# A decoder layer on one core: keys projected already turned, halves exchanged by DMA, and scores clipped by VectorE ahead of the exponential

## The chip, the core and the metric

The kernel runs on one core of one Trainium2 chip. TensorE (PE) multiplies matrices and writes to PSUM, eight banks of 512 fp32 numbers for each of 128 partitions. VectorE (DVE) and ScalarE (ACT) read and write PSUM and SBUF, GpSimd (POOL) only SBUF, and SyncE (SP) issues most of the transfers between memories. Each engine works through its own list of instructions in order and waits at semaphores for the others. The metric is the device time of one execution in microseconds; less is better.

## The reference

One decoder layer on x of 4 batches x 256 tokens x 128 features: local attention with relative positions, cross attention to a context of 512 tokens per batch, and a mixture of 12 experts, each added to x. The change touches the cross attention alone, which is, with 16 heads of 64:

```
lat = layer_norm(x);  ctx = layer_norm(context)          # with learned gain and bias
q = lat @ Wq;  k, v = split(ctx @ Wkv)                   # 16 heads of 64
k = concat([k1 * cos - k2 * sin, k2 * cos + k1 * sin])   # k1, k2: the halves of a head's 64
attn = clip(q @ k.T * 64 ** -0.5, -11, 11)
out = softmax(attn) @ v
x = x + out @ Wo + bo
```

## The kernel before

The program is written by hand, engine by engine, and the order of each engine's list is the order of the code. After the local attention comes a loop of 32 **rounds**, one for each pair of heads of a batch (8 pairs in each of 4 batches). In all engines' code the round is `r`, and a pair `p` has two halves of the context, `i = 2p` and `2p + 1`.

In round r, TensorE computes the scores of the *next* pair (`scores(2r+2)`, `scores(2r+3)`, two PSUM banks each, 128 x 1024 numbers), projects one **value unit** (128 context tokens x 8 heads, three matmuls of 512 columns, bank 5), in even rounds projects queries for the next two pairs (`queries`), weights the values by this pair's exponentials (`weigh_values(2r)`, `weigh_values(2r+1)`), sums the exponentials with a matrix of ones (`sum_weights(r)`), and projects one **key unit** (128 context tokens x 8 heads). Some rounds have an extra: the turn of a new batch's context or latents (the normed x), or an output projection (`project`). The value units run four ahead of the round in which they are first needed.

Keys arrive with tokens on the partitions. VectorE multiplies them from PSUM by cos and, halves swapped, by sin (`key_unit`, three instructions), GpSimd adds the two (`key_sum`), TensorE turns four 128 x 128 blocks for each pair (`turn_keys`) and ScalarE copies the result out of PSUM as `kT` (`keys_turned`). Queries, contexts, latents, projections and turned keys all share bank 6 (`MISC_BANK`), one after the other, with the semaphores `misc_ps` (written) and `misc_read` (read).

The scores go from PSUM through ScalarE, which writes their exponential to SBUF (`exponent`), and VectorE limits that in place (`clip`). GpSimd adds the halves of the exponentials (`weights_summed`, `halves_summed`). VectorE's `divide(r-1)` takes the reciprocal of the sums of the pair before and multiplies the weighted values by it. In VectorE's list, each round begins with it:

```
for r in range(NPAIR):
    if r:
        divide(r - 1)
    ...
    if r + 1 < NPAIR:
        clip(2 * r + 2)
        clip(2 * r + 3)
```

Between the division and the clips stand, in a few rounds, the statistics and normalizing of the next batch's latents (`latents`) and of the last norm (`final_norm`). After the loop come the experts, which the change leaves as they are.

Of the kernel before, what the change touches and what calls it, by code (L numbers as in the profile page):

```python
# [23 lines left out]
def decoder_layer(nc, x, ctx_in, pos, a_wq, a_wk, a_wv, a_wpost, a_wrel, a_pds,  # L24
# [52 lines left out]
    E_LO, E_HI = float(np.exp(-11.0)), float(np.exp(11.0))  # L77
    K_LEAD, V_LEAD = 2 * KC - 1, KC
# [21 lines left out]
    with ExitStack() as ctx:  # L100
# [17 lines left out]
        WARM_BANK, WARM_FIRST, WARM_NEXT = 6, 10, 4  # L118
# [21 lines left out]
        def bank(i, parts=P):  # L140
# [24 lines left out]
        ctx_sb = sb("ctx_sb", [P, NCT, D], F32, cross)  # L165
        ctx_f = sb("ctx_f", [P, SC], F32, cross)
# [3 lines left out]
        rope_a = sb("rope_a", [P, 2, GC], F32, cross)  # L170
        rope_b = sb("rope_b", [P, 2, GC], F32, cross)
        wkv_hi = sb("wkv_hi", [P, 2 * HX * DX], F32R, cross)
        wkv_lo = sb("wkv_lo", [P, 2 * HX * DX], F32R, cross)
        cos_sb = sb("cos_sb", [P, KC, DX // 2], F32, cross)
        sin_sb = sb("sin_sb", [P, KC, 2, DX // 2], F32, cross)
        k_rot = [sb(f"k_rot{i}", [P, KC, GC], F32, cross) for i in range(2)]
        raws = [raw[:, 0, :], raw[:, 1, :]] + [k_rot[1][:, t, :] for t in range(KC)]
# [29 lines left out]
        oT = sb("oT", [P, WALL * CH], F32, first)  # L207
        first.close()
# [9 lines left out]
        kT = sb("kT", [P, 3, SC], F32, second)  # L218
# [50 lines left out]
            rstd_done xn_done absneg_done softplus_done qscale_done awT_ps awT_done xT_ps xT_done v_tok_ps v_tok_done pad_set v_zeroed v_padded v_stored v_spread0 v_spread1 v_spread2  # L269
            rel_ps relM_done q_ps k_ps qM_done kM_done bd_ps bd_raw_done added_done pT_ps pT_done logit_ps  # L270
            capped_done prob_done oa_ps rq_done oq_done oT_ps oT_done ya_ps x1_done w_hi_done w_lo_done ctxn_done sin_done
            ct_ps ctx_f_done ctx_hi_done ctx_lo_done unit_ps rope_done v_done
            xn1_done lat_in_done lat_ps lat_f_done lat_hi_done lat_lo_done             k_rot_done misc_ps misc_read score_ps exp_done
            clip_done part_done es_done pv_ps den_ps rden_done ox_done tail_ps x2_done ld_w0 ld_w1 ld_w2 ld_w3
            ld_pw ld_u ld_b2 wt_done wt_hi_done wt_lo_done rt_ps rt_done fn_done fT_ps fT_done addr_ps addr_done z_ps
# [11 lines left out]
        UNIT = [("k", n) for n in range(KC)] + [("v", 0), ("v", 1), ("k", KC), ("k", KC + 1), ("v", 2), ("v", 3), ("k", KC + 2)]  # L287
        UNIT_BANK = [7, 6, 7, 6, 7, 6, 7, 6, 7, 7, 5]
        ROUND_VALUES, ROUND_KEYS = {}, {}
        for r in range(NPAIR):  # L290
            if r + V_LEAD < NG * KC:
                ROUND_VALUES[r] = len(UNIT)
                UNIT.append(("v", r + V_LEAD))
            if r + K_LEAD < NG * KC:
                ROUND_KEYS[r] = len(UNIT)
                UNIT.append(("k", r + K_LEAD))
        UNIT_BANK += [5] * (len(UNIT) - len(UNIT_BANK))

        def bank_before(m):

            n = m - 1
            while n >= 0 and UNIT_BANK[n] != UNIT_BANK[m]:
                n -= 1
            return n

        LATENT_ROUNDS = {1: (0, 1, 2), 2: (9, 10, 11), 3: (14, 15, 16)}
        CONTEXT_ROUND = {0: 1, PPB - 2: 2, 2 * PPB - 2: 3}
# [7 lines left out]
        MISC_BANK = 6  # L315
        MISC = [("keys", 0), ("queries", 0), ("keys", 1), ("keys", 2)]
        for r in range(NPAIR):
            if r in CONTEXT_ROUND:
                MISC.append(("context", CONTEXT_ROUND[r]))
            if r % 2 == 0 and r // 2 + 1 < NQ:  # L320
                MISC.append(("queries", r // 2 + 1))
            if r in extras:
                MISC.append(extras[r])
            if r + 3 < NPAIR:
                MISC.append(("keys", r + 3))
        MISC_NO = {what: n for n, what in enumerate(MISC)}

# [4 lines left out]
        def pv_bank(p):  # L332
# [4 lines left out]
        LAST_KEYS, LAST_VALUES = NG * KC - 1 - K_LEAD, NG * KC - 1 - V_LEAD  # L337
        NORM_ROUND = (B - 1) * PPB - 2
        ROUTE = {"weights": 2 * NORM_ROUND, "tokens": 2 * NORM_ROUND + 2, "address": 2 * NORM_ROUND + 4, "scores": 2 * NORM_ROUND + 6,
                 "chosen": 2 * NORM_ROUND + 8, "softmax": 2 * NORM_ROUND + 10, "turn": 2 * NORM_ROUND + 12}  # L340
        ROUTE_READ = {"weights": ("rt_done", 2), "tokens": ("fT_done", 1), "address": ("addr_done", 1), "scores": ("z_done", 1)}
# [33 lines left out]
        def _(sp):  # L375
# [24 lines left out]
            sp.dma_start(cos_sb[:, :, :], rope_cos.rearrange("(t p) d -> p t d", p=P)).then_inc(s["ld_rope"], 16)  # L400
            sp.dma_start(sin_sb[:, :, 1, :], rope_sin.rearrange("(t p) d -> p t d", p=P)).then_inc(s["ld_rope"], 16)
# [32 lines left out]
            sp.dma_start(pw_sb[:, :], f_pw).then_inc(s["ld_pw"], 16)  # L434
            for i, u in enumerate((f_u1, f_u2, f_u3)):
                sp.dma_start(u_sb[i * NE:(i + 1) * NE, :], u).then_inc(s["ld_u"], 16)
# [19 lines left out]
            for n in range(2 * NE):  # L456
                for g in GATE_AT.get(n, ()):
                    if GLOADS[g][1] == 1:
                        store_gates(GLOADS[g][0])
                    load_gates(g)  # L460
                if n >= RING:
                    sp.wait_ge(s["wt_done"], n - RING + 1)
                for j in range(P // SQ):
# [7 lines left out]
                    sp.dma_start(dst, src).then_inc(s[f"ld_w{n % RING}"], 16)  # L471
            for t in range(NT):
# [6 lines left out]
        def _(pool):  # L479
# [23 lines left out]
            link(pool.tensor_tensor(mask4[:, :], mask8[:, 0:G], mask8[:, G:HA], ALU.add))  # L503
            pool.memset(v_pad[:, :, 0:DA], 0.0).then_inc(s["pad_set"], 1)
# [8 lines left out]
            rstd_of(LN_C, KC)  # L513
            pool.memset(bd[:, :, :], 0.0).then_inc(s["consts"], 1)
# [13 lines left out]
            def key_sum(k):  # L528

                g, t = divmod(k, KC)  # L530
                pool.wait_ge(s["rope_done"], k + 1)
                if g >= 2:
                    pool.wait_ge(s["misc_ps"], MISC_NO["keys", GP * (g - 1) - 1] + 1)
                pool.tensor_tensor(k_rot[g % 2][:, t, :], rope_a[:, k % 2, :], rope_b[:, k % 2, :], ALU.add).then_inc(s["k_rot_done"], 1)  # L534

            def weights_summed(i):

                p, half = divmod(i, 2)
                pool.wait_ge(s["clip_done"], i + 1)
# [12 lines left out]
            weight_rest(1)  # L552
            key_sum(0)
            key_sum(1)
            weight_rest(2)
            key_sum(2)
            weight_rest(3)
            key_sum(3)
# [10 lines left out]
            for k in range(KC, KC + 2):  # L569
                key_sum(k)  # L570
# [18 lines left out]
            key_sum(K_LEAD - 1)  # L589
            for r in range(NPAIR):  # L590
# [10 lines left out]
                if r in ROUND_KEYS:  # L601
                    key_sum(r + K_LEAD)
# [27 lines left out]
        def _(act):  # L630
            act.dma_start(x_sb[:, NT // 2:NT, :], x[B // 2:B].rearrange("b (t p) d -> p (b t) d", p=P)).then_inc(s["ld_x1"], 16)
            act.dma_start(pds_b[:, 0, :], a_pds.partition_broadcast(P)).then_inc(s["ld_pds"], 16)
            act.dma_start(pos_sb[:, :], pos).then_inc(s["ld_pos"], 16)
            act.preload_act_table(ACT.Exp)
# [13 lines left out]
            act.wait_ge(s["absneg_done"], 1)  # L648
# [12 lines left out]
            act.wait_ge(s["qscale_done"], 1)  # L661
# [27 lines left out]
            def context_f(b):  # L689
                if b >= 1:  # L690
                    act.wait_ge(s["ctx_lo_done"], b)
                act.activation(ctx_f[:, :], bank(7 if b == 0 else MISC_BANK), ACT.Identity, scale=affine[:, 2:3], bias=affine[:, 3:4])\
# [49 lines left out]
            for i in range(2):  # L742
                shift_positions(act, 1, i)
            value_unit(4)
# [133 lines left out]
            for r in range(NPAIR):  # L878
# [18 lines left out]
                if r + 3 < NPAIR:  # L897
                    keys_turned(r + 3)
# [943 lines left out]
```

## Time and profile before

| | us |
|---|---|
| median of three runs | 442.74 (442.21 to 443.37) |
| the profiled execution | 443.53 |
| its span, first to last instruction | 441.6 |

| engine | busy us | share of the span | instructions |
|---|---|---|---|
| TensorE | 423.2 | 96% | 3210 |
| VectorE | 325.0 | 74% | 686 |
| ScalarE | 195.5 | 44% | 312 |
| GpSimd | 257.4 | 58% | 225 |

The durations further down come from the profiled execution. Its time is that of the whole execution, and the span is what the profiler saw of it. Matmuls overlap in TensorE's pipeline, so the time that a group of them takes is read from the starts of neighbouring groups. An engine's idle time counts only where something that ends later waits for it.

### The profile page before, as it was taken

The numbers are of one execution on the slowest core, as the hardware profiler recorded it, in microseconds if no ns is written. First come the engines' busy times: TensorE is split into PE (matmuls) and PEld (weight loads), VectorE is DVE, ScalarE is ACT, GpSimd is POOL, SyncE is SP. The second block draws the span as 40 slices with busy tenths as digits, with TensorE's granted clock in tenths as the row PEclk, the third lists the DMA queues.
The fourth block names the chain that finished last, engine by engine and source line by source line (L and its number), as shares of the span: only waits on it lengthen the run. The fifth ranks groups of instructions, "written<-read, shape, count | busy, mean of one in ns | idle before, by whom it ended". The sixth has DMA issues, their size and how long they took to land.

```text
span 441.6 us, 8547 instructions
## 1 busy us (share of the span) xinstructions
PE 423.2 (96%) x3210; PEld 313.1 (71%) x3210; DVE 325.0 (74%) x686; ACT 195.5 (44%) x312; POOL 257.4 (58%) x225
## 2 busy tenths in 40 slices
PE   8988799999999999999999999999999999999996
PEld 8666666676667766767776666768767788888885
DVE  8998658978869767985777698797687861755554
ACT  6848364646455346362535554534437634000000
POOL 5858238998778867878769665677524850000000
PEclk9999999999999999999999999999999999999999
DMA  7766405000000000000000000435518660000000
GB/s 178 202 150 90 85 18 87 1 0 1 1 1 1 1 1 1 1 0 1 2 1 1 1 1 1 154 63 94 122 29 212 143 98 0 6 7 12 6 7 13
DMA packets 75434, 19.85 MB, mean 45 GB/s; under 512 B 66741, under 2 KB 73834, under 8 KB 75394
## 3 DMA queue, kind: packets, MB, share of 16 engines
q1 hardware_dynamic: 72628, 18.27, 19.6%
q10 hardware_dynamic: 2766, 1.04, 1.1%
q8 instruction: 26, 0.43, 0.4%
q14 instruction: 14, 0.11, 0.1%
HBM read 17.27 MB, written 2.02 MB: 44 GB/s over the span
## 4 chain that ended last, share of the span: by engine, by line
PE 76%; DVE 11%; ACT 5%; issue 4%; DMA 1%; ACTq 1%; POOL 1%; DVEq 0%; POOLq 0%
PE psum L1199 11%; PE psum L1182 11%; PE psum L992 9%; PE psum L1382 5%; PE psum L1383 5%; PE psum L1381 5%; PE psum L1341 4%; PE psum L1342 4%; PE psum L1343 4%; PE psum L1218 3%; PE psum L1209 3%; PE psum L1101 3%; PE psum L941 1%; ACT e_sb L806 1%; DVE rden L1607 1%
## 5 line engine op out<-in xcount | busy, mean ns | idle before, releaser
L542 POOL TENSOR_TENSOR e_part<-e_sb 128x512 f32<-128x512 f32 x64 | 89.1, 1410 | 42.1 <-DVE e_sb L1600 30.4
L806 ACT ACTIVATE e_sb<-psum 128x1024 f32<-128x1024 f32 x64 | 62.2, 1022 | 16.7 <-PE psum L1182 16.7
L1182 PE MATMUL psum<-q_t,kT 64*128 64x256 f32 x512 | 64.2, 389 | 0.0
L1199 PE MATMUL psum<-e_sb,v_sb 128*64 128x256 f32 x512 | 63.8, 386 | 0.0
L1806 DVE SCALAR_TENSOR_TENSOR x_sb<-psum,dw,x_sb 128x128 f32<-128x128 f32 x96 | 33.7, 351 | 37.4 <-PE psum L1383 34.8
L1607 DVE RECIPROCAL rden<-psum 128x256 f32<-128x256 f32 x32 | 55.8, 1745 | 0.2 <-PE psum L1209 0.2
L1600 DVE TENSOR_SCALAR e_sb<-e_sb 128x1024 f32<-128x1024 f32 x64 | 51.4, 839 | 3.8 <-ACT e_sb L806 3.8
L1182 PEld LDWEIGHTS psum<-q_t,kT 64*128 64x128 f32 x512 | 46.7, 186 | 9.6 <-issue 5.0
L785 ACT ACTIVATE kT<-psum 128x512 f32<-128x512 f32 x32 | 19.1, 598 | 77.7 <-PE psum L1101 77.3
L1199 PEld LDWEIGHTS psum<-e_sb,v_sb 128*64 128x64 f32 x512 | 33.7, 136 | 22.3 <-issue 6.6
L534 POOL TENSOR_TENSOR k_rot<-rope_a,rope_b 128x512 f32<-128x512 f32 x32 | 41.7, 1307 | 12.8 <-DVE rope_b L1487 12.8
L582 POOL TENSOR_TENSOR xeT_lo<-xeT,xeT_hi 128x512 fp32r<-128x512 f32 x24 | 31.6, 1318 | 28.0 <-ACT xeT_hi L820 27.9
L1482 DVE TENSOR_TENSOR rope_a<-psum,cos_sb 128x512 f32<-128x512 f32 x32 | 22.1, 690 | 28.8 <-PE psum L992 26.6
L548 POOL TENSOR_TENSOR e_part<-e_part 128x512 f32<-128x512 f32 x32 | 41.4, 1293 | 2.5
L1341 PE MATMUL psum<-xeT_hi,w1T_hi 128*128 128x512 f32 x96 | 38.9, 405 | 0.8 <-ACT h_f L926 0.5
L1382 PE MATMUL psum<-w2T_lo,h_hi 128*128 128x512 f32 x96 | 38.0, 396 | 0.0
L1383 PE MATMUL psum<-w2T_hi,h_lo 128*128 128x512 f32 x96 | 37.8, 394 | 0.0
L1343 PE MATMUL psum<-xeT_hi,w1T_lo 128*128 128x512 f32 x96 | 37.5, 390 | 0.0
L1342 PE MATMUL psum<-xeT_lo,w1T_hi 128*128 128x512 f32 x96 | 37.5, 390 | 0.0
L1381 PE MATMUL psum<-w2T_hi,h_hi 128*128 128x512 f32 x96 | 37.3, 389 | 0.0
L992 PE MATMUL psum<-wkv_hi,ctx_hi 128*128 128x512 f32 x64 | 31.5, 493 | 2.8 <-DVE rope_b L1487 2.7
L820 ACT ACTIVATE xeT_hi<-xeT 128x512 fp32r<-128x512 f32 x24 | 15.2, 631 | 28.7 <-DVE xeT L1647 21.3
(195 smaller groups left out, 780.8 us busy)
## 6 DMA issues: line engine op xcount, KB each, us to landing
w_raw<-in_L_ffn_W_dram SPq DMA_DIRECT2D x96, 64.0 KB, 2.4
gates<-gate_dram SPq DMA_DIRECT2D x6, 768.0 KB, 4.9
ctx_sb<-in_ctx_dram SPq DMA_DIRECT2D x4, 256.0 KB, 6.2
vbd<-v_dram SPq DMA_DIRECT2D x16, 52.6 KB
v_dram<-v_tok SPq DMA_DIRECT2D x4, 136.0 KB, 3.3
raw<-in_L_xattn_Wkv_dram SPq DMA_DIRECT2D x2, 256.0 KB, 4.5
k_rot<-in_L_xattn_Wkv_dram SPq DMA_DIRECT2D x2, 256.0 KB, 5.3
k_rot<-in_L_xattn_Wq_dram SPq DMA_DIRECT2D x2, 256.0 KB, 5.7
```

The source lines that it names most:

```text
L542: pool.tensor_tensor(e_part[:, p % 2, half, :, :], e_sb[:, i % ERING, :, 0, :], e_sb[:, i % ERING, :, 1, :], ALU.add)\
L806: act.activation(e_sb[:, i % ERING, :, :, :].rearrange("p a k t -> p (a k t)"), psum[:, a:a + 2, :].rearrange("p a b -> p (a b)"), ACT.Exp ...
L992: mm = pe.matmul(o, c, w_[:, wc:wc + GC], start=(part == 0), stop=(part == 2))
L1182: mm = pe.matmul(psum[:, 2 * (i % 2) + a, t * S:(t + 1) * S], kT[rows, p % 3, kt * P:(kt + 1) * P], q_t[rows, j % 2, p % 2, :], start=True ...
L1199: mm = pe.matmul(psum[DX * a:DX * a + DX, pv_bank(p), 0:S], v_sb[g % 2][:, kt, 2 * pp + a, :], e_sb[:, i % ERING, a, t, :], start=(kt == 0 ...
L1341: pe.matmul(bank(c), w1T_hi[:, e, c, :], hi, start=(e == 0), stop=False)
L1342: pe.matmul(bank(c), w1T_hi[:, e, c, :], lo, start=False, stop=False)
L1343: mm = pe.matmul(bank(c), w1T_lo[:, e, c, :], hi, start=False, stop=(e == NE - 1))
L1381: pe.matmul(o, hi, w_hi, start=(c == 0), stop=False)
L1382: pe.matmul(o, hi, w_lo, start=False, stop=False)
L1383: mm = pe.matmul(o, lo, w_hi, start=False, stop=(c == HC - 1))
L1607: dve.reciprocal(rden[:, p % 2, :], psum[:, pv_bank(p), S:2 * S]).then_inc(s["rden_done"], 1)
```

## The change

Keys. A key unit is now one pair of heads x 512 context tokens, with the weights as the stationary operand, so that PSUM receives the keys already turned. The tables of cos and sin are turned once at the start (`rope_t`, 32 small transposes). VectorE makes both products in one instruction of 1024 numbers (`key_products`). The sin product has to move to the other half of each head, which is now another partition: for the first four pairs TensorE does that with a permutation matrix and VectorE adds (`first_key_sum`), and for the other 28 four DMAs on SP's queue do it, and GpSimd adds into `kT`, a ring of four (`key_sum`). The turns of keys and ScalarE's copies of them are gone.

Scores. VectorE clips the scores from PSUM into SBUF, and ScalarE takes the exponential there in place.

Banks. Key units of the loop use bank 6. Queries, contexts, latents and projections use bank 5, where the value units are (`aside`, two of them excepted).

```diff
-    K_LEAD, V_LEAD = 2 * KC - 1, KC
+    S_CLIP = 11.0 / X_SCALE
+    K_LEAD, V_LEAD = 4, KC
+    KRING = 4
...
+                VALUES_BEFORE[what] = min(r + 1 + V_LEAD, NG * KC)
...
+            def swap_keys(p):
+
+                sp.wait_ge(s["rope_done"], 2 + p + 1)
+                sp.wait_ge(s["k_done"], p - 1)
+                for q in range(2 * DX // QD):
+                    to = q ^ 1
+                    sp.dma_start(raw[QD * to:QD * (to + 1), p % 2, :], rope[QD * q:QD * (q + 1), p % 2, 1, :]).then_inc(s[f"ld_raw{p % 2}"], 16)
...
             def exponent(i):
-                act.wait_ge(s["score_ps"], i + 1)
...
+                act.wait_ge(s["clip_done"], i + 1)
+                e = e_sb[:, i % ERING, :, :, :].rearrange("p a k t -> p (a k t)")
+                act.activation(e, e, ACT.Exp, scale=X_SCALE).then_inc(s["exp_done"], 1)
...
             for r in range(NPAIR):
                 if r + 1 < NPAIR:
                     exponent(2 * r + 2)
+                if ASIDE[r] and r in ROUND_VALUES:
+                    value_unit(ROUND_VALUES[r])
+                if r + 1 < NPAIR:
                     exponent(2 * r + 3)
+                if not ASIDE[r] and r in ROUND_VALUES:
+                    value_unit(ROUND_VALUES[r])
+                for what in ASIDE[r]:
+                    aside(what)
...
                 if MISC_NO[what]:
                     pe.wait_ge(s["misc_read"], MISC_NO[what])
+                if what in VALUES_BEFORE:
+                    pe.wait_ge(s["v_done"], VALUES_BEFORE[what])
...
+                    unit_values(ROUND_VALUES[r])
+                if r in ROUND_KEYS:
+                    unit_keys(ROUND_KEYS[r])
+                for what in ASIDE[r]:
+                    aside(what)
+                route_1(2 * r)
                 weigh_values(2 * r)
...
             def clip(i):
 
-                dve.wait_ge(s["exp_done"], i + 1)
-                e = e_sb[:, i % ERING, :, :, :].rearrange("p a k t -> p (a k t)")
-                dve.tensor_scalar(e, e, E_LO, E_HI, ALU.max, ALU.min).then_inc(s["clip_done"], 1)
+                dve.wait_ge(s["score_ps"], i + 1)
...
+                a = 2 * (i % 2)
+                dve.tensor_scalar(e_sb[:, i % ERING, :, :, :].rearrange("p a k t -> p (a k t)"), psum[:, a:a + 2, :].rearrange("p a b -> p (a b)"),
+                                  -S_CLIP, S_CLIP, ALU.max, ALU.min).then_inc(s["clip_done"], 1)
```

How this moves instructions is shown at three places. `v_done` counts the value units that ScalarE has copied out. First TensorE's list from the end of one round into one with a query projection (`q_t` of L1115 before, L1157 after), before the change:

```order
L992 MATMUL psum<-wkv_hi,ctx_lo 128x512
L1101 MATMUL psum<-ident,k_rot 128x128 [waits misc_read,k_rot_done]
L1101 MATMUL psum<-ident,k_rot 128x128 x3
L1182 MATMUL psum<-q_t,kT 128x256 [waits exp_done,misc_read]
L1182 MATMUL psum<-q_t,kT 128x256 x3
L1182 MATMUL psum<-q_t,kT 128x256 [waits exp_done]
L1182 MATMUL psum<-q_t,kT 128x256 x3
L992 MATMUL psum<-wkv_hi,ctx_hi 128x512 [waits ctx_lo_done,rope_done]
L992 MATMUL psum<-wkv_lo,ctx_hi 128x512
L992 MATMUL psum<-wkv_hi,ctx_lo 128x512
L1115 MATMUL psum<-lat_hi,wq_hi 128x256 [waits misc_read,lat_lo_done]
```

and the same place after it (L1010 to L1012 is the value unit, L1031 to L1033 the key unit):

```order
L1226 MATMUL psum<-q_t,kT 128x256 [waits clip_done,k_done,misc_read]
L1226 MATMUL psum<-q_t,kT 128x256 x3
L1226 MATMUL psum<-q_t,kT 128x256 [waits clip_done]
L1226 MATMUL psum<-q_t,kT 128x256 x3
L1010 MATMUL psum<-wkv_hi,ctx_hi 128x512 [waits ctx_lo_done,misc_read,v_done]
L1011 MATMUL psum<-wkv_lo,ctx_hi 128x512
L1012 MATMUL psum<-wkv_hi,ctx_lo 128x512
L1031 MATMUL psum<-ctx_hi,wkv_hi 128x512 [waits ctx_lo_done,rope_done]
L1032 MATMUL psum<-ctx_hi,wkv_lo 128x512
L1033 MATMUL psum<-ctx_lo,wkv_hi 128x512
L1157 MATMUL psum<-lat_hi,wq_hi 128x256 [waits v_done,misc_read,lat_lo_done]
```

The four turns of keys are gone, the key unit stands behind the value unit, and the query projection has a new wait, for `v_done`. Second, ScalarE's list in two rounds, the second with a query projection, before:

```order
L806 ACTIVATE e_sb<-psum 128x1024 [waits part_done,pv_ps,score_ps] x2
L713 ACTIVATE v_sb<-psum 128x512 [waits pv_ps,unit_ps]
L785 ACTIVATE kT<-psum 128x512 [waits score_ps,misc_ps]
L806 ACTIVATE e_sb<-psum 128x1024 [waits part_done,pv_ps,score_ps] x2
L713 ACTIVATE v_sb<-psum 128x512 [waits pv_ps,unit_ps]
L798 ACTIVATE q_t<-psum 128x512 [waits score_ps,misc_ps]
L785 ACTIVATE kT<-psum 128x512 [waits score_ps,misc_ps]
```

and after (each `e_sb` is an exponential, `v_sb` the copy of a value unit):

```order
L811 ACTIVATE e_sb<-e_sb 128x1024 [waits clip_done]
L730 ACTIVATE v_sb<-psum 128x512 [waits pv_ps,unit_ps]
L811 ACTIVATE e_sb<-e_sb 128x1024 [waits clip_done]
L806 ACTIVATE q_t<-psum 128x512 [waits score_ps,misc_ps]
L811 ACTIVATE e_sb<-e_sb 128x1024 [waits clip_done]
```

The copy of the value unit now stands between the two exponentials of the round, and these wait for clips, where they waited for scores. Third, VectorE's list of one round, before:

```order
L1607 RECIPROCAL rden<-psum 128x256 [waits ox_done,den_ps]
L1611 TENSOR_TENSOR o_t<-psum,rden 128x256 [waits rden_done]
L1600 TENSOR_SCALAR e_sb<-e_sb 128x1024 [waits exp_done] x2
L1482 TENSOR_TENSOR rope_a<-psum,cos_sb 128x512 [waits k_rot_done,unit_ps]
L1487 TENSOR_TENSOR rope_b<-psum,sin_sb 128x8x32 x2
```

and after (`den_ps` counts TensorE's `sum_weights`):

```order
L1662 RECIPROCAL rden<-psum 128x256 [waits ox_done,den_ps]
L1666 TENSOR_TENSOR o_t<-psum,rden 128x256 [waits rden_done]
L1654 TENSOR_SCALAR e_sb<-psum 128x1024 [waits part_done,pv_ps,score_ps] x2
L1531 TENSOR_TENSOR rope<-psum,rope_t 128x1024 [waits k_done,unit_ps]
L1662 RECIPROCAL rden<-psum 128x256 [waits ox_done,den_ps]
```

The places are the same, but the clips now come between the scores and the exponentials, and one instruction stands where the three products of keys stood.

## Rows read from the trace of the kernel before

**Rows 1.** The page, busy time, share of the span and instructions of TensorE.

```profile
PE 423.2 (96%) x3210; PEld 313.1 (71%) x3210; DVE 325.0 (74%) x686; ACT 195.5 (44%) x312; POOL 257.4 (58%) x225
```

**Rows 2.** Windows, rounds 0 to 27: length, engines' busy time in their order, granted clock, DMA.

```profile
60.72:270.75 210.03, 205.00 (x1482) 142.41 (x1482) 166.82 (x295) 105.71 (x154) 166.74 (x132) 1.00 0.04 6
```

**Rows 3.** The chain that ended last: start, us, what.

```profile
60.72 1.06 PE psum L1182 x8
...
145.35 1.98 PE psum L1218 x16
...
270.75 1.93 PE psum L1182 x16
```

**Rows 4.** Timeline of a round without extras, all engines.

```profile
97.65 0.69 DVE L1482 TENSOR_TENSOR rope_a<-psum,cos_sb 128x512 f32<-128x512 f32 x1 [1.69 <-PE psum L992]
...
97.98 2.00 PE L1182 MATMUL psum<-q_t,kT 64*128 64x256 f32 x16
...
98.92 1.75 DVE L1607 RECIPROCAL rden<-psum 128x256 f32<-128x256 f32 x1
99.17 1.94 ACT L806 ACTIVATE e_sb<-psum 128x1024 f32<-128x1024 f32 x2 [0.48 <-PE psum L1182]
...
99.91 0.50 PE L992 MATMUL psum<-wkv_hi,ctx_hi 128*128 128x512 f32 x1
...
100.71 0.42 DVE L1611 TENSOR_TENSOR o_t<-psum,rden 128x256 f32<-128x256 f32 x1
...
100.79 1.95 PE L1199 MATMUL psum<-e_sb,v_sb 128*64 128x256 f32 x16
...
100.99 0.60 ACT L713 ACTIVATE v_sb<-psum 128x512 f32<-128x512 f32 x1
101.05 1.28 DVE L1600 TENSOR_SCALAR e_sb<-e_sb 128x1024 f32<-128x1024 f32 x2
...
102.57 0.60 PE L1209 MATMUL psum<-e_part,ones 128*64 128x256 f32 x4
...
103.10 0.50 PE L992 MATMUL psum<-wkv_hi,ctx_hi 128*128 128x512 f32 x1
...
104.43 2.00 PE L1182 MATMUL psum<-q_t,kT 64*128 64x256 f32 x16
```

**Rows 5.** Timeline of a round with a query projection, TensorE: its start and what follows.

```profile
122.08 0.28 PE L1115 MATMUL psum<-lat_hi,wq_hi 128*128 128x256 f32 x1
...
122.88 1.95 PE L1199 MATMUL psum<-e_sb,v_sb 128*64 128x256 f32 x16
```

**Rows 6.** Line L1600: count, duration min/median/max in ns, first and last start.

```profile
L1600 DVE TENSOR_SCALAR e_sb<-e_sb x64: 660/685/2229, 57.4 to 287.7; 128x1024 f32<-128x1024 f32 x64
```

**Rows 7.** Groups by line: count, us in all, mean ns, idle before.

```profile
L1496 DVE TENSOR_SCALAR kM<-psum,mask 128x512 f32<-128x512 f32 x8 | 8.5, 1185 | 1.0 <-PE psum L963 1.0
```

**Rows 8.** Timeline of a round with a context turn.

```profile
107.44 0.78 ACT L692 ACTIVATE ctx_f<-psum,affine 128x512 f32<-128x512 f32 x1
...
108.36 0.36 PE L1115 MATMUL psum<-lat_hi,wq_hi 128*128 128x256 f32 x1 [0.64 <-ACT ctx_f L692]
...
108.92 1.56 DVE L1472 TENSOR_TENSOR ctx_lo<-ctx_f,ctx_hi 128x512 fp32r<-128x512 f32 x1
```

**Rows 9.** The chain at the last sums of the loop.

```profile
294.00 0.58 PE psum L1209 x4
```

**Rows 10.** Timeline of VectorE behind these sums.

```profile
294.63 1.76 DVE L1607 RECIPROCAL rden<-psum 128x256 f32<-128x256 f32 x1
```

**Rows 11.** Timeline of VectorE's work for the latents in one round.

```profile
176.25 0.59 DVE L1425 TENSOR_SCALAR xn<-x_sb,mv,rstd 128x128 f32<-128x128 f32 x2
...
177.56 1.26 DVE L1600 TENSOR_SCALAR e_sb<-e_sb 128x1024 f32<-128x1024 f32 x2
```

**Rows 12.** DMA issues: count, KB each, median us from issue to landing.

```profile
w_raw<-in_L_ffn_W_dram SPq DMA_DIRECT2D x96, 64.0 KB, 2.4
```

More of the change, by code:

```diff
@@ L551, in _ @@
             weight_rest(0)
[L552 to L558, printed above, removed]
+            for n in range(1, 4):
+                weight_rest(n)
             pool.wait_ge(s["added_done"], 1)
@@ L633, in _ @@
             act.dma_start(pos_sb[:, :], pos).then_inc(s["ld_pos"], 16)
+            for i, table in enumerate((rope_cos, rope_sin)):
+                act.dma_start(rope_in[:, i, :, :], table.rearrange("(t p) d -> p t d", p=P)).then_inc(s["ld_rope"], 16)
             act.preload_act_table(ACT.Exp)
@@ L875, in route_1, with aside @@
                     if ROUTE[stage] == i:
-                        route(0, stage, 5)
+                        route(0, stage, ROUTE_BANK.get(stage, 5))
+            def aside(what):
+                if what[0] == "context":
+                    misc_wait(what)
+                    context_f(what[1])
+                elif what[0] == "queries":
+                    queries_out(what[1])
+                elif what[0] == "latents":
+                    misc_wait(what)
+                    latents_f(what[1])
             for r in range(NPAIR):
@@ L893, in _ @@
                     final_normalize(0)
-                if r in extras and extras[r][0] == "latents":
-                    misc_wait(extras[r])
-                    latents_f(extras[r][1])
-                if r + 3 < NPAIR:
-                    keys_turned(r + 3)
+                for what in LATE[r]:
+                    aside(what)
                 route_1(2 * r + 1)
@@ L951, in _ @@
             turned(psum[:, 1, P:P + NPOS], pos_sb[:, :], NPOS).then_inc(s["awT_ps"], 1)
+            pe.wait_ge(s["ld_rope"], 32)
+            for i in range(2):
+                for t in range(KC):
+                    for q in range(2 * DX // QD):
+                        mm = turned(psum[QD * q:QD * (q + 1), 5 - i, t * P:(t + 1) * P], rope_in[:, i, t, :])
+                mm.then_inc(s["rope_ps"], 1)
             keep_clock(WARM_NEXT)
@@ L996, in relative, with swap_keys @@
+            def swap_keys(p):
+                if p == 0:
+                    pe.wait_ge(s["turn_set"], 2 * DX // QD + 2)
+                pe.wait_ge(s["rope_done"], 2 + p + 1)
+                pe.matmul(bank(UNIT_BANK[p]), swap[:, :], rope[:, p % 2, 1, :], start=True, stop=True).then_inc(s["rope_ps"], 1)
             def relative(c):
@@ L1289, in route_1, with aside @@
                     pe.wait_ge(s["rt_done"], 2)
+                if i == ROUTE["turn"]:
+                    pe.wait_ge(s["rope_done"], 2 + NPAIR)
                 for stage in ROUTE:
                     if ROUTE[stage] == i:
-                        route(0, stage, 5)
+                        route(0, stage, ROUTE_BANK.get(stage, 5))
+            def aside(what):
+                if what[0] == "queries":
+                    queries(what[1])
+                    return
+                misc_free(what)
+                if what[0] == "context":
+                    turn_context(what[1], 5, "misc_ps")
+                elif what[0] == "latents":
+                    turn_latents(what[1], 5, "misc_ps")
+                else:
+                    project(what[1], what[2], psum[:, misc_bank(what), 0:D]).then_inc(s["misc_ps"], 1)
             for r in range(NPAIR):
```

372 lines of the change are left out of this document (181 added, 191 removed).

## The prediction

> **What bounds the kernel now.** I read the page first. TensorE (PE) is busy 96% of the span, 423.2 us [rows 1], so the question for any stretch is whether something makes TensorE wait there. Next I cut the span at the starts of two score groups on the chain of waits, scores 2 at 60.72 and scores 58 at 270.75 [rows 3]. Between them lie rounds 0 to 27 of the cross attention, the rounds that the change touches most. They take 210.03 us, TensorE is busy 205.0 of them, VectorE (DVE) 166.8, and the granted clock is 1.00, the upper level of 2.4 GHz [rows 2]. So TensorE sets the pace there, and VectorE has about a fifth to spare.
>
> Then I read one round in the timeline [rows 4]. A round without extras runs from 97.98 to 104.43, 6.45 us: scores 1.93, a value unit until 100.79 (0.88 with the switch of operands), weighting by the exponentials 1.78, the two sums 0.53, a key unit and its four turns 1.33. What matters most here is who waits for whom. ScalarE (ACT) starts its exponentials at 99.17, as soon as scores are in PSUM. VectorE divides (reciprocal from 98.92), multiplies (100.71) and only then clips (101.05), but nobody needs those clips before the next round. So VectorE's slow reciprocal is on nobody's way. A round with a query projection has 0.80 more (122.08 to 122.88, [rows 5]).
>
> **The change, part by part.**
>
> *Removed from TensorE.* The key unit moves beside the value unit, and the four turns of keys go. A round without extras becomes 1.93 + 0.88 + 0.8 + 1.78 + 0.53, about 5.9 us instead of 6.45 [rows 4]: 0.6 us in each of 28 rounds, some 17 us, if nothing waits. ScalarE's copy of keys leaves its queue, and nothing waits for that space.
>
> *Clips from PSUM.* A clip of 1024 numbers in SBUF takes 685 ns in the median [rows 6]. From PSUM I go by two rows: a product of 256 numbers takes 0.42 us (100.71) and one of 512 takes 0.69 (97.65, both [rows 4]), so 0.27 us for each 256 more, and 1.23 us for 1024. The bounds are 0.685 below, and above twice the 1185 ns that the tensor-scalar operation from PSUM takes for 512 with a scattered output [rows 7], about 2.3 us. I take 1.24, because the new output is contiguous like that of the product. The Trainium skill, "VectorE: DVE Perf Modes", section "Mode 2×_2P — use both read ports for one tensor", says that the two-port mode which doubles a single-source operation is open only to SBUF, since VectorE has one read port on PSUM. By its rate of one element per cycle at 0.96 GHz, 1024 numbers are an estimated 1.1 us before overhead; with that the forecast below would be about 3 us lower. No row shows this very operation.
>
> *Key products and sums.* One product of 1024 from PSUM (1.24) stands for three that took from 97.65 to 98.92, 1.27 [rows 4]: nothing to count. GpSimd (POOL) adds as before.
>
> *Halves exchanged by DMA.* Four transfers of 64 KB per pair go through SP's queue. A 64 KB transfer lands 2.4 us after its issue [rows 12]; even four in sequence, 9.6 us, end inside the more than ten that lie between a key product late in one round and its sum at the end of GpSimd's next round. I count 0. What covers it is the four-slot ring of keys; with that cover gone it would be some 2 us a round. Expert loads behind it on SP wait for the end of the loop anyway.
>
> *The wait that is added.* The query projection (also a context turn, a latent turn or an output projection) now writes bank 5, where this round's value unit has just been put. So it waits for ScalarE's copy of that unit. In ScalarE's queue the copy stands behind the first exponential; that waits for the clip; and the clip stands behind the division in VectorE's queue, which waits for the sums at the end of TensorE's last round. Counted from the start of a round's scores:
> the reciprocal starts at 0.05 (294.58 to 294.63, [rows 9, 10]); the multiply 1.79 later; the clip 0.34 after that [rows 4]; 1.24 for the clip; 0.05 to hand over; 0.96 until ScalarE takes up its next instruction (half of 1.94, less overlap, [rows 4], with 0.04 for the SBUF source, an estimate); 0.60 for the copy, like the value copy at 100.99 [rows 4]; 0.14 until TensorE starts (context copy 107.44 + 0.78, then 108.36, [rows 8]). Together 5.17 us. TensorE itself is there at 1.93 + 0.88 + 0.8 = 3.6. It waits 1.6 us, and behind it in its queue are the weighting and the sums of this round, for which the next division waits. So the chain closes on itself once a round, and a round costs 5.17 + the extra + 1.78 + 0.53 = 7.48 + the extra.
>
> The sum over rounds 0 to 27:
> - 23 rounds with such an extra: 23 x 7.48 = 172.0.
> - The extras: 13 query projections x 0.80 = 10.4; three contexts and three latents x 0.4 (an estimate) = 2.4; five output projections x 1.98 [rows 3] = 9.9.
> - Round 0, taken like the others: 7.5. Rounds 5 and 9, without an extra: 11.7.
> - Rounds 23 and 25: a routing step waits for the value copy, which there stands behind both exponentials: 7.48 + 0.96 + 0.9 each, 18.7.
> - Work on VectorE ahead of the clips, now on the chain: statistics or normalizing of latents in seven of these rounds and once for the last norm. One such piece takes 176.25 to 177.56, 1.31 [rows 11]; 8 x 1.3 = 10.4. Until now VectorE's spare fifth held it.
> - Work behind the clips that waits for ScalarE or TensorE and so delays the next division: three contexts (first copy to remainder 1.48, then 0.7 to 1.56, [rows 8], and the key product, ending near 9.5 where the round ends at 8), three latents, two routing rounds: 8 x 1.5 = 12.0, the softest term.
>
> That is 255.0 against 210.0, +45. The time ahead of the loop: 64 small transposes of tables and four fp32 swaps come, six filler matmuls, seven key units' sums and a negation go; I take +1, bounds -2 and +3, since much of that stretch waits on DMA round trips. The rounds after 270.75 and the experts (156 us) are the same. So +46 on the profiled execution's 443.53 us gives 489.5; that execution lies 0.8 above the median of the three runs (442.74), so I predict **489 us**.
>
> **The rivals.**
> *Faster.* The copies come early enough and TensorE never waits. Then only the removed work shows: 255 less 23 x 1.6, 2 x 2.5 and the 22.4 of late work is 191, 19 less than now, and the time about 425 us. For it: TensorE is 97.6% busy in the loop [rows 2], and its removed work is real. Against: the copy would have to end by 3.6 us, and the reciprocal and multiply alone, 2.2 us [rows 4], with the exponential and the copy, 1.56, pass that without any clip. It decides only if the division does not stand ahead of the clip, which the order shows it does.
> *About the same.* The waits are half as long as I count (a clip at the SBUF price, and the late work mostly in gaps): 45 less 14 less 22 still leaves +9, so this needs two errors of mine together. 442 us.
> *Slower still, the clock.* In the loop the granted clock is 1.00 [rows 2], and the longest TensorE wait that my rows show is 0.64 us [rows 8]. With the change TensorE would wait 1.6 us in most rounds and 3 us in the seven with latents work. If the clock fell to its lower level (1.2 GHz) in those seven, their TensorE work of at most 6.3 us would double, up to +44; for half of each, +22, so about 510 us. The Trainium skill, "TensorE: Matmul & The Clock Gate", the table in "Why this matters for your kernels", says that idle gaps between bursts of matmuls bring the half rate back; no row of this loop shows one, so I give it little.
>
> **How the numbers follow.** Forecast (chain through the value copy) 0.83; clock on top 0.06; faster 0.08; same 0.03. A measurement of this kernel can tell about 0.3% from no change. Faster 0.08, same 0.03, slower 0.89. The range: a clip at 0.685 takes 25 x 0.55 = 14 off, late work half hidden 11; a clip at 2.3 adds 26; the clock adds 22. I take 468 to 510, which leaves out the faster and same cases and the outer ends.
>
> **What would show it.** Right: in the profile after, TensorE idle before the query projection with ScalarE's value copy as the releaser, 1.5 us or more, some 20 times; query rounds of 8.2 to 8.5 us; the reciprocal starting within 0.2 us of the sums; clips of 1.2 us; VectorE idle at the end of rounds; the turns of keys gone. Wrong: TensorE still over 95% busy in the loop; clips waiting for scores instead of for the division; copies released early; or waits at the key sums, which would mean that the DMA is late.

## The result, and the profile after

The changed kernel takes **518.4 us** (516.3 to 520.9, four runs) where the kernel before takes 442.6: 1.172 times as long (95% interval 1.169 to 1.175). The forecast was 489, with a range to 510. The profiled execution took 517.46 us, its span 515.7, 74.1 more than before. The page of the changed kernel, engines' busy times (to be read beside [rows 1]) and TensorE's granted clock in 40 slices of the span:

```profile
PE 437.1 (85%) x3148; PEld 316.1 (61%) x3148; DVE 339.6 (66%) x627; ACT 179.2 (35%) x280; POOL 238.4 (46%) x227
...
PEclk9899989789987898989999798899999999999999
```

TensorE is busy 85% of the span instead of 96%, and it does fewer matmuls for 14 us more of busy time, since part of them run at less than full clock. Windows of the changed kernel (columns as in [rows 2]): rounds 0 to 27, round 28, and the rest; then single rounds, 4, 5, 6 and 10.

```profile
66.43:339.09 272.66, 215.57 (x1376) 144.97 (x1375) 177.28 (x244) 91.56 (x127) 154.15 (x133) 0.91 0.13 31
339.09:349.82 10.73, 7.37 (x49) 4.45 (x47) 5.12 (x5) 3.77 (x5) 5.00 (x5) 0.84 0.10 25
349.82:515.70 165.88, 159.46 (x766) 124.86 (x764) 105.97 (x245) 46.34 (x80) 52.09 (x40) 1.00 0.30 64
```

```profile
104.73:115.44 10.71, 8.35 (x50) 5.53 (x48) 6.45 (x6) 3.09 (x4) 7.25 (x6) 0.84 0.20 50
115.44:121.26 5.82, 5.82 (x44) 3.86 (x42) 5.58 (x5) 2.24 (x3) 1.18 (x1) 1.00 0.01 1
121.26:129.63 8.37, 6.77 (x50) 4.63 (x48) 6.17 (x6) 3.45 (x5) 7.51 (x7) 1.00 0.18 46
154.48:168.76 14.28, 9.60 (x50) 6.05 (x48) 8.70 (x12) 4.08 (x6) 10.44 (x10) 0.77 0.15 38
```

The 74.1 us lie in three places: 5.7 ahead of the loop (66.43 less 60.72), 62.6 in rounds 0 to 27 (272.66 less 210.03), and 5.8 behind them. In the loop the granted clock is 0.91 where it was 1.00. Rounds 5 and 6, at a clock of 1.00, take 5.82 and 8.37, as forecast (5.9, and 7.48 + 0.80). Rounds 4 and 10, like round 6 with a query projection, take 10.7 and 14.3 at 0.84 and 0.77.

Round 6 in the timeline, to be read beside [rows 4, 5]:

```profile
121.26 2.00 PE L1226 MATMUL psum<-q_t,kT 64*128 64x256 f32 x16
121.38 1.76 DVE L1662 RECIPROCAL rden<-psum 128x256 f32<-128x256 f32 x1 [0.20 <-PE psum L1253]
...
123.51 2.34 DVE L1654 TENSOR_SCALAR e_sb<-psum 128x1024 f32<-128x1024 f32 x2
...
124.76 1.06 ACT L811 ACTIVATE e_sb<-e_sb 128x1024 f32<-128x1024 f32 x1 [3.14 <-DVE e_sb L1654]
125.72 0.58 ACT L730 ACTIVATE v_sb<-psum 128x512 f32<-128x512 f32 x1
...
126.45 0.36 PE L1157 MATMUL psum<-lat_hi,wq_hi 128*128 128x256 f32 x1 [1.60 <-ACT v_sb L730]
...
127.32 1.95 PE L1243 MATMUL psum<-e_sb,v_sb 128*64 128x256 f32 x16
```

This is the chain of the forecast, link by link: sums, reciprocal, multiply, clip, exponential, value copy, query projection. It takes 126.45 - 121.26 = 5.19 us (forecast 5.17), and TensorE waits 1.60. Round 10 in the timeline, where the normalizing and statistics of latents stand ahead of the clips:

```profile
162.75 0.55 PE L1157 MATMUL psum<-lat_hi,wq_hi 128*128 128x256 f32 x1 [4.68 <-ACT v_sb L730]
...
164.30 3.68 PE L1243 MATMUL psum<-e_sb,v_sb 128*64 128x256 f32 x16
...
167.77 1.07 PE L1253 MATMUL psum<-e_part,ones 128*64 128x256 f32 x4
...
168.88 1.76 DVE L1662 RECIPROCAL rden<-psum 128x256 f32<-128x256 f32 x1 [5.60 <-PE psum L1253]
```

TensorE waits 4.68 us, and behind the wait the same weighting that took 1.95 us in round 6 takes 3.68, and the sums 1.07 instead of 0.60: TensorE runs at its lower level. VectorE waits 5.60 us for these sums, so the chain, which closes on itself, carries the delay into the next round.

Groups by line of the changed kernel (busy us, mean ns, idle before), and last the transfers of the exchange (count, KB each, median us from issue to landing):

```profile
L811 ACT ACTIVATE e_sb<-e_sb 128x1024 f32<-128x1024 f32 x64 | 67.4, 1054 | 184.5 <-DVE e_sb L1654 184.0
L1662 DVE RECIPROCAL rden<-psum 128x256 f32<-128x256 f32 x32 | 56.1, 1754 | 61.8 <-PE psum L1253 61.7
L1654 DVE TENSOR_SCALAR e_sb<-psum 128x1024 f32<-128x1024 f32 x64 | 75.1, 1212 | 1.0 <-PE psum L1226 0.9
L1531 DVE TENSOR_TENSOR rope<-psum,rope_t 128x1024 f32<-128x1024 f32 x32 | 38.7, 1213 | 1.1 <-PE psum L1033 1.1
L557 POOL TENSOR_TENSOR kT<-rope,raw 128x512 f32<-128x512 f32 x28 | 35.5, 1269 | 0.0
...
raw<-rope SPq DMA_DIRECT2D x112, 64.0 KB, 2.0
```

Clips (1.21 us) and key products (1.21) cost what was forecast, and GpSimd never waits for the exchange by DMA (idle 0.0 ahead of the key sums). ScalarE waits 184 us for clips.

What remains open is the 17.6 us of the loop beyond the forecast's 45, and the 11.5 outside it. **Theory:** the chain is as long as forecast, and the rest of the loop's loss is the clock that falls behind the waits. **Rivals:** the chain itself is longer than the sum of its rows (work on VectorE ahead of it), and the low clock costs nothing, as TensorE waits anyway; VectorE is simply too full; or the keys part has a wait of its own.

### The profile page after: what moved, and what is told of

The parts are those of the page before. It is cut to its first block, busy times and chain, and to the rows that moved or that the text cites. A ratio compares the mean times of both kernels' runs of the same rounds, so it can differ in the third digit from the quotient of the medians.

```text
span 515.7 us, 8442 instructions
## 1 busy us (share of the span) xinstructions
PE 437.1 (85%) x3148; PEld 316.1 (61%) x3148; DVE 339.6 (66%) x627; ACT 179.2 (35%) x280; POOL 238.4 (46%) x227
## 4 chain that ended last, share of the span: by engine, by line
PE 58%; DVE 23%; issue 10%; ACT 7%; DMA 1%; SPq 0%; DVEq 0%; POOL 0%
PE psum L1243 11%; DVE rden L1662 7%; DVE e_sb L1654 6%; PE psum L1428 4%; PE psum L1429 4%; PE psum L1427 4%; PE psum L1226 4%; PE psum L1387 4%; PE psum L1262 3%; PE psum L1389 3%; PE psum L1388 3%; PE psum L1253 3%; ACT v_sb L730 2%; ACT e_sb L811 2%; PE psum L1157 2%
## 5 line engine op out<-in xcount | busy, mean ns | idle before, releaser
L565 POOL TENSOR_TENSOR e_part<-e_sb 128x512 f32<-128x512 f32 x64 | 82.0, 1288 | 122.9 <-ACT e_sb L811 109.4
L811 ACT ACTIVATE e_sb<-e_sb 128x1024 f32<-128x1024 f32 x64 | 67.4, 1054 | 184.5 <-DVE e_sb L1654 184.0
L1243 PE MATMUL psum<-e_sb,v_sb 128*64 128x256 f32 x512 | 77.0, 452 | 1.3 <-issue 1.2
L1654 DVE TENSOR_SCALAR e_sb<-psum 128x1024 f32<-128x1024 f32 x64 | 75.1, 1212 | 1.0 <-PE psum L1226 0.9
L1243 PEld LDWEIGHTS psum<-e_sb,v_sb 128*64 128x64 f32 x512 | 40.0, 159 | 27.0 <-issue 14.0
L1531 DVE TENSOR_TENSOR rope<-psum,rope_t 128x1024 f32<-128x1024 f32 x32 | 38.7, 1213 | 1.1 <-PE psum L1033 1.1
L1157 PE MATMUL psum<-lat_hi,wq_hi 128*128 128x256 f32 x32 | 11.7, 366 | 31.6 <-ACT v_sb L730 31.5
L557 POOL TENSOR_TENSOR kT<-rope,raw 128x512 f32<-128x512 f32 x28 | 35.5, 1269 | 0.0
L1157 PEld LDWEIGHTS psum<-lat_hi,wq_hi 128*128 128x128 f32 x32 | 7.1, 222 | 38.0 <-issue 36.8
L1262 PE MATMUL psum<-wo_sb,o_t 128*128 128x128 f32 x128 | 17.8, 299 | 10.5 <-issue 10.5
```

The lines of the kernel that those rows point to most:

```text
L565: pool.tensor_tensor(e_part[:, p % 2, half, :, :], e_sb[:, i % ERING, :, 0, :], e_sb[:, i % ERING, :, 1, :], ALU.add)\
L811: act.activation(e, e, ACT.Exp, scale=X_SCALE).then_inc(s["exp_done"], 1)
L1243: mm = pe.matmul(psum[DX * a:DX * a + DX, pv_bank(p), 0:S], v_sb[g % 2][:, kt, 2 * pp + a, :], e_sb[:, i % ERING, a, t, :], start=(kt == 0 ...
L1654: dve.tensor_scalar(e_sb[:, i % ERING, :, :, :].rearrange("p a k t -> p (a k t)"), psum[:, a:a + 2, :].rearrange("p a b -> p (a b)"), -S_C ...
```

## The experiments

**The value copy first** (e1).

```diff
-                if r + 1 < NPAIR:
-                    exponent(2 * r + 2)
-                if ASIDE[r] and r in ROUND_VALUES:
+                if r in ROUND_VALUES:
                     value_unit(ROUND_VALUES[r])
                 if r + 1 < NPAIR:
+                    exponent(2 * r + 2)
                     exponent(2 * r + 3)
-                if not ASIDE[r] and r in ROUND_VALUES:
-                    value_unit(ROUND_VALUES[r])
```

> One edit: in every round ScalarE copies the value unit before its two exponentials. Theory A (the loss is the chain through the value copy, division - clip - exponential - copy): TensorE finds bank 5 free at 3.6 us of a round, the wait of 1.6 us at the asides goes, and with it the drops of the granted clock that follow it; rounds of 6 us and 6.8 with a query, bound by TensorE and VectorE together (2.1 + 2.4 + 1.2 = 5.8 us of VectorE), loop 205 to 215 instead of 272.7, time 450 to 460. Rival B (VectorE is simply too full: clips of 1.21 from PSUM on top of the division, whoever waits for the copy): no change, 510 to 520. Rival C (the clock falls for another reason than the wait): TensorE's wait goes, but rounds at a clock of 0.7 to 0.87 stay, time near 480.

464.0 us (1.047, 1.043 to 1.051); loop 217.05, clock 0.98. The wait at the asides is gone, and 55.6 us of the loop's 62.6 with it, though VectorE does the same work: VectorE's load is not the main cause. The time is 4 us over what was expected. About 2 us of that lie in the loop, where a smaller wait took the place of the first, and the loop also starts 1.8 us later than in the changed kernel (68.21, against 66.43). The scores of this kernel in its groups by line (busy us, mean ns, idle before, and what ended it):

```profile
L1223 PE MATMUL psum<-q_t,kT 64*128 64x256 f32 x512 | 67.4, 404 | 11.0 <-ACT q_t L806 11.0
```

They wait 11.0 us, in seven rounds, for ScalarE's copy of the queries. It stands behind the second exponential, and so behind the second clip and the division; the next scores need it.

**The clips first** (e2).

```diff
+                if r + 1 < NPAIR:
+                    clip(2 * r + 2)
+                    clip(2 * r + 3)
                 if r:
                     divide(r - 1)
...
-                if r + 1 < NPAIR:
-                    clip(2 * r + 2)
-                    clip(2 * r + 3)
```

> One edit: in every round VectorE does both clips before the division (and the latents' statistics behind the division), ScalarE's order as in the changed kernel. Theory A: the division leaves the chain; clip 1 ends at 2.3 us of a round, the exponential at 3.3, the copy at 3.9, TensorE starts the aside at 4.05 instead of 5.2, being there at 3.6; loop 215 to 225, time 450 to 465, some 5 us more than with the copy first if nothing else differs, less if the work that stands ahead of the clips matters more. Rival B (VectorE too full): no change, since the same work stays in its queue, 510 to 520.

460.4 us (1.040, 1.035 to 1.045); loop 219.45, clock 0.98. With the division off the chain, the query projection waits for the value copy only 9.9 us in 15 rounds, 0.5 to 0.6 in most, as worked out.

**The keys part alone** (e3), with exponential and clip as in the kernel before; scores and weighting wait accordingly.

```diff
             def exponent(i):
-                act.wait_ge(s["clip_done"], i + 1)
+                act.wait_ge(s["score_ps"], i + 1)
...
             def clip(i):
-                dve.wait_ge(s["score_ps"], i + 1)
+                dve.wait_ge(s["exp_done"], i + 1)
```

> The keys part alone: keys projected turned and rotated from PSUM, exchanged by DMA, as in the changed kernel, but scores as before (exponential by ScalarE from PSUM, clip by VectorE in SBUF behind it). Theory A: the exponential no longer waits for the division, the copy ends at 3.5 us of a round, no wait; TensorE saves the turns of keys, 0.6 us a round; loop about 195, and with the 5.7 us lost ahead of the loop the time is 430 to 437, faster than the kernel before. Rival D (the keys part brings its own wait, at the DMA exchange or at bank 5): 450 or more, with waits at the scores for the key sums or at the asides.

**437.7 us, 0.988 (0.986 to 0.991): 1.2% less than before.** Windows, rounds 0 to 27, and round 27 alone:

```profile
65.34:264.73 199.39, 194.09 (x1376) 133.26 (x1375) 172.89 (x244) 91.77 (x127) 167.44 (x133) 0.99 0.18 43
```

```profile
252.44:264.73 12.29, 9.60 (x61) 6.90 (x59) 9.15 (x13) 2.54 (x3) 7.52 (x6) 0.86 0.15 38
```

The loop is 10.6 us shorter than before; in rounds 0 to 26 no wait of TensorE is longer than 0.73 us, and none is for the key sums or the DMA. So the loss of the whole change is that of the scores part. The time is just above the 430 to 437 expected, because of round 27, taken up below.

**The scores part alone** (e4), the kernel before with the reverse of that edit.

> The scores part alone: the kernel before with VectorE's clip from PSUM ahead of ScalarE's exponential in SBUF, keys as before. Theory A: the value copy stands behind both exponentials there and the key unit waits for it in bank 5, while VectorE's key products stand ahead of the next division; round of 2.2 + 2.4 + 1.05 + 0.75 + 0.65 + 1.3 = 8.4 us, loop 240 to 260 instead of 210, time 475 to 495. Rival D (the loss comes from the keys part or from its order of asides): near 443 to 450.

520.2 us (1.175, 1.172 to 1.178), as much as the whole change. A round with neither extra nor latents work takes 8.38 us, against 8.4 worked out; in the timeline of one (136.80 to 145.18) the key unit waits:

```profile
143.20 0.58 ACT L713 ACTIVATE v_sb<-psum 128x512 f32<-128x512 f32 x1
143.84 0.50 PE L988 MATMUL psum<-wkv_hi,ctx_hi 128*128 128x512 f32 x1 [1.82 <-ACT v_sb L713]
```

But the loop takes 282.7 at a clock of 0.90, far over the 240 to 260 expected, and the time misses its 475 to 495: here too the plain rounds come out and the rounds with long waits do not. How much of that is the waits themselves and how much the clock was not measured in this kernel.

**Both orders** (e5), the edits of e1 and e2 together.

> Both orders at once: ScalarE copies the value unit before the exponentials, and VectorE clips before it divides; the clip stays from PSUM. Each order alone left a wait of its own: with the copy first the next scores waited 1.3 to 2.5 us for ScalarE's copy of the queries (which stands behind the second exponential, behind the second clip, behind the division); with the clips first the asides waited 0.5 us for the value copy. Theory A (the chain): with both neither is left, query rounds of 6.85 us, loop 200 to 208 against 217.1 and 219.5, time 446 to 452. Rival B (a clip from PSUM ahead of the exponential has a price of its own, in VectorE's time, whatever the order): rounds stay at 7 us or more, time 456 or more.

449.8 us (1.018, 1.014 to 1.021); loop 207.20. Query rounds take 6.86 us, the same as with the keys part alone, where the clip is in SBUF and late. A clip from PSUM ahead of the exponential therefore costs nothing in a plain round once the orders suit it.

**TensorE kept at work while it waits** (e6). Repeats of a key unit's first matmul, 4 to 19 in each of 25 rounds (`FILL`), stand ahead of it; the unit then overwrites the bank.

```diff
+                for _ in range(FILL.get(p - K_LEAD, 0)):
+                    pe.matmul(o, wkv_hi[:, cols], ctx_hi[:, b % 2, :], start=True, stop=True)
                 pe.matmul(o, wkv_hi[:, cols], ctx_hi[:, b % 2, :], start=True, stop=False)
```

> The changed kernel with TensorE kept at work while it waits: ahead of the key unit of each of 25 rounds stand 4 to 19 repeats of its first matmul (0.22 us each, results overwritten by the unit), chosen to fill the measured wait of that round but for some 0.4 us. The chain through the value copy is left as it is. Theory C (beyond the chain, the loop lost 18 us because TensorE's granted clock falls after the waits and the projections, weightings and sums behind them run at half rate): the rounds that showed a clock of 0.72 to 0.87 show 0.95 or more and lose 1 to 3 us each; loop 252 to 257 instead of 272.7, which is the 255 that the chain gives; time 497 to 503, although 200 matmuls more are done. Rival A' (the chain alone is longer than counted, and the low clock costs nothing, since TensorE waits anyway): 515 to 522, no change.

**500.3 us (1.132, 1.130 to 1.134), 18 less than the changed kernel, with 200 matmuls more.** Windows, rounds 0 to 27, and rounds 4, 5, 6 and 10:

```profile
66.52:319.81 253.29, 239.69 (x1575) 170.98 (x1574) 178.42 (x244) 91.63 (x127) 154.38 (x133) 0.99 0.14 33
```

```profile
101.97:111.10 9.13, 8.81 (x59) 6.33 (x58) 6.54 (x6) 3.10 (x4) 5.70 (x5) 1.00 0.18 44
111.10:116.93 5.83, 5.83 (x45) 3.86 (x43) 5.58 (x5) 2.26 (x3) 2.75 (x3) 1.00 0.10 24
116.93:125.31 8.38, 7.93 (x56) 5.57 (x54) 6.18 (x6) 3.44 (x5) 7.51 (x7) 1.00 0.19 47
148.47:159.97 11.50, 11.08 (x70) 8.20 (x68) 8.84 (x12) 4.10 (x6) 8.97 (x9) 1.00 0.14 34
```

Rounds 4 and 10 come back to a clock of 1.00 and get shorter by 1.6 and 2.8 us; rounds 5 and 6, at 1.00 already, don't change by more than 0.01. The eleven rounds that get shorter by over 0.2 us (2, 4, 8, 10, 11, 13, 16, 22, 23, 25, 26) give 19.3 of the 19.4 between the two loops, and they are the rounds from 1 on in which the clock had fallen. The other 17 change by at most 0.04, though 14 of them hold repeats too, so the repeats do nothing where the clock was up. The loop that is left, 253.3 us, is the chain at a clock of 0.99 (only round 0 is still at 0.80), where the forecast had 255.0. This settles the loop: the rival, that the low clock costs nothing, would have shown no change.

**Two orders mended on the keys part alone** (e7): ahead of the loop, VectorE's statistics ahead of its table copies and GpSimd's clearing ahead of the swap matrix; in the loop:

```diff
-                if i in ROUTE.values():
+                if i in (ROUTE[stage] for stage in ROUTE if stage not in ("chosen", "softmax")):
                     pe.wait_ge(s["v_done"], min(r + 1 + V_LEAD, NG * KC))
                     pe.wait_ge(s["misc_read"], MISC_BEFORE[r] + len(ASIDE[r]))
```

> The keys part alone, with two orders mended. Ahead of the loop VectorE takes the statistics of the first context before its copies of the turned tables, and GpSimd clears its buffers before it makes the swap matrix; in the loop TensorE no longer waits at the two routing steps in which it has no work. Theory (the 5.7 us ahead of the loop come from the context's statistics and GpSimd's clearing coming late, so that the normalizing of the context meets GpSimd's work; and the 2.65 us of wait in round 27, with a clock of 0.86 behind it, come from that routing wait): the loop starts 2 to 3 us earlier than with the keys part alone, at 62 to 63.5 instead of 65.34, round 27 takes 8.5 to 9.5 instead of 12.29, time 431 to 434. Rival (the start is bound by the 64 transposes of the tables on TensorE; round 27 is bound by VectorE's routing work): 436 to 438.

433.0 us (0.981, 0.978 to 0.984). The profiled execution is the shortest of its four (428.9), so the mends were also run apart.

**The start alone** (e9), **the routing wait alone** (e10), each on the keys part.

> The keys part alone with only the two orders ahead of the loop mended (statistics of the first context ahead of the table copies, buffers cleared ahead of the swap matrix); the routing wait stays. With both mends the profiled execution, the shortest of its kernel (428.9 against a median of 433.0), started its loop at 61.50 instead of 65.34. Theory (these orders cost 2.5 us at turn_context, from 20.0 to 22.5): the context is turned 1.5 to 2.5 us earlier, the loop starts at 62 to 64, time 434 to 436. Rival (what starts the loop later stands behind, at the wait for the value copy near 40 us): the context is turned earlier, the loop starts at 65 as before, time 437 to 438.

> The keys part alone without the wait of TensorE at the two routing steps in which it has no work; the orders ahead of the loop stay. Theory: round 27 takes 8 instead of 12.29, the rest is as with the keys part alone; time 433 to 434. Rival: the wait goes to the next user of that PSUM bank, the value unit of round 28, and 437 stays.

The start alone: 436.4 us (0.986, 0.982 to 0.990), an interval that overlaps that of the keys part alone, so no gain is shown. The context is turned at 20.53 instead of 22.51, but the loop starts at 65.72, no earlier (e3: 65.34): in between, VectorE waits 2.65 us for a DMA of shifted positions where it waited 0.91. The routing wait alone: **433.4 us, 0.979 (0.976 to 0.982), 2.1% under the kernel before**, which is all that both mends gave. Window of round 27:

```profile
250.81:258.75 7.94, 7.89 (x60) 5.69 (x59) 7.80 (x20) 2.54 (x3) 5.07 (x5) 1.00 0.13 34
```

It takes 7.94 us instead of 12.29. There TensorE had waited 2.65 us at a stage in which only VectorE works, for a read of bank 5 that stands behind that work, and in e3 the weighting behind it ran at half rate. It did not in e9, behind the same wait, and the round took 10.59. The weighting in e3 and in e9:

```profile
260.73 3.31 PE L1247 MATMUL psum<-e_sb,v_sb 128*64 128x256 f32 x16 [2.65 <-issue]
```

```profile
261.31 1.95 PE L1247 MATMUL psum<-e_sb,v_sb 128*64 128x256 f32 x16 [2.65 <-issue]
```

**The whole change with all orders mended** (e8), the edits of e5 and e7 together.

> The whole change, scores part included, with all the orders mended at once: value copy ahead of the exponentials, clips ahead of the division, the two orders ahead of the loop, and no wait at routing steps in which TensorE has no work. Theory (the change loses by four orders, not by what its instructions cost): the 449.8 us of both orders together less 3.8 ahead of the loop (65.34 to 61.50 with the keys part alone), less 5.5 in round 27 (14.00 to 8.5) and 2 in round 28; 437 to 441, faster than the kernel before by about 1%, but behind the keys part alone with its orders mended (433), since VectorE's clips stay ahead of TensorE in the rounds with latents and routing work. Rival (the waits of rounds 23, 26 and 27 are VectorE's load there, not the routing wait): 444 or more.

446.7 us (1.009, 1.006 to 1.011): the expectation of 437 to 441 fell. Its loop is 200.95, but round 23 waits 2.51 us for ScalarE's copy of the routing weights, and a routing turn in round 28 waits 3.65, with a clock of 0.72 for that round, 11.95 us long. So in rounds with routing work the scores part still brings waits of its own, and of that part nothing was found that pays for it: with it the time is 446.7, without it, with the same two mends, 433.0 (e7).

## Why the prediction was wrong, by its steps

*Removed from TensorE.* Right: 5.82 us for a plain round (5.9), and alone this part makes the kernel 1.2% faster (e3).

*Clips from PSUM; key products; DMA.* Right: 1.21 us each, as counted (1.24), and the exchange is hidden (64 KB in 2.0 us). The estimate from the Trainium skill, "VectorE: DVE Perf Modes", section "Mode 2×_2P — use both read ports for one tensor", left out overhead and was 0.1 short; its rule agrees with the trace, in which the clip from PSUM takes 1.21 us and the clip in SBUF 0.69 (the median of [rows 6]).

*The wait that is added.* Right, in mechanism and size, where VectorE has no other work: in round 6 5.19 us from the start of the round to the projection (5.17), 1.60 us of wait. e1 and e2 each take one link out, and the wait goes or shrinks to 0.5. The rival "faster" (a loop of 191 us) comes near the keys part alone (199.39); what it needed, a copy that doesn't wait for the division, is what the scores part takes away.

*The sum over rounds 0 to 27.* Right at full clock: 253.3 measured in e6, 255.0 forecast. That it came so close is luck in part. The terms for late work were not measured apart, and single rounds were off by over 2 us either way, which cancels: for round 13 7.48 + 1.98 gives 9.5, and 11.9 came; for round 25 7.48 + 0.96 + 0.9 + 1.5 gives 10.8, and 8.7 came.

*The rival "slower still, the clock".* **This is the step that failed.** It named the mechanism and worked out 22 us, and then gave it 0.06, because "no row of this loop shows one". But that loop had no long waits to show: the longest was 1.06 us (round 0; the 0.64 is only the longest among the rows), and the forecast itself put waits of 1.6 and 3 us into it. It happened, and cost 19.4 us (272.66 less 253.29), in rounds spread over the loop and not only in those with latents.

In the changed kernel the granted clock stays at 1.00 behind the waits of 1.6 us (rounds 6 and 12), falls behind those of 2.36, 2.56, 3.06 and 4.68 (rounds 4, 8, 2 and 10), and does not behind those of 2.24 and 2.35 (rounds 14 and 18). The length of the wait alone does not decide it here: the clock stays up behind 2.85 us (rounds 1 and 15) and falls in the rounds of 1.78 and 2.00 us (25 and 11). Even the same wait goes both ways, as in e3 and e9 above. Ahead of the loop the first local values wait 2.82 us in all ten profiles with the new keys; they then take 2.2 us in four of them and 2.6 to 3.9 in six. The changed kernel (granted clock 1.00 in these values) and e3 (0.54):

```profile
43.99 2.21 PE L1106 MATMUL psum<-vbd,prT 96*32 96x68 f32 x128 [2.82 <-ACT v_sb L730]
```

```profile
42.66 3.74 PE L1110 MATMUL psum<-vbd,prT 96*32 96x68 f32 x128 [2.82 <-ACT v_sb L730]
```

So 19.4 us is what the clock cost in the profiled execution of the changed kernel, and not a fixed price of its waits. The Trainium skill, "TensorE: Matmul & The Clock Gate", section "Why this matters for your kernels", says that idle gaps bring the half rate back. The trace agrees: in eleven rounds from 1 on the clock fell behind waits, though not behind every long one. The rule should have weighed more than the absence of falls from a loop without long gaps.

*Ahead of the loop, +1.* Measured +5.7, outside the bounds of -2 and +3; the transposes of the tables, which the prediction counts as 64, are 32. The places are seen, the shares aren't: the first context is turned 2.5 us later (20.04 to 22.53), the local values wait 2.82 us for a value copy where they waited 1.62 for something else, and the last project waits 1.51 for ScalarE behind a clip, against 0.21 with the keys part alone. Of these e9 mended the first without a shorter start, so it alone does not set it. The cause stays open.

*Rounds 28 on, the same.* Measured +5.8; 4.3 of it is round 28 (10.73, 6.4 before), where a routing turn waits 3.4 us, at a clock of 0.84. The other 1.5 stays open. With the keys part alone this stretch is only 0.5 longer than before, so most of it comes with the scores part.

Chain 43.3, clock 19.4, ahead 5.7 and behind 5.8 make the 74.1 (rounded). The clock alone, on top of the forecast, would have given 489 + 19 = 508; it is the clock together with the time outside the loop that makes 518.

## What to carry to other kernels

When a sum of rows puts waits like those of this case (1.3 to 4.7 us) into a stage in which TensorE had none, work out what follows at half clock too, as part of the forecast, and as a range, since the same wait can leave the clock up or not: here it was 19 us on top of 43. Before an operation is moved to another engine's list, look at what stands ahead of it there and who needs its result this round; the clip cost no more time than forecast, but it tied ScalarE's copies to VectorE's division. And try the parts of a change apart: one of the two gains 1.2% (2.1% with one needless wait taken out), and the other loses 17%.

## What the runs showed that was not expected

Doing more made the kernel faster: 200 matmuls whose results are thrown away, in time in which TensorE waited, took 18 us off. And a chain that closes on itself once a round passes on most of what a low clock costs, although TensorE is busy only 79% of the loop (215.57 of 272.66): in round 10 VectorE waits 5.60 us for sums that TensorE makes at half rate, and at full clock the round is 2.8 us shorter (e6). Round 26 is the exception: at full clock TensorE only waits longer for the value copy there (2.05 us instead of 1.30), and the round is just 0.25 us shorter.
